# Decoder block, two layers: softmax sums on TensorE, one exponential per bank, layer normalisation on ScalarE

## The reference, cut to what matters

```python
def _layernorm(x, axis=-1, eps=1e-05):
    m = jnp.mean(x, axis=axis, keepdims=True)
    v = jnp.var(x, axis=axis, keepdims=True)
    return (x - m) / jnp.sqrt(v + eps)

# third block ("pick"): the 50 tokens with the largest gate attend to each other, 16 heads of 16
scores = jnp.einsum('bqhd,bkhd->bhqk', q, k) / jnp.sqrt(jnp.float32(dh))
attn = jax.nn.softmax(scores, axis=-1)
o = jnp.einsum('bhqk,bkhd->bqhd', attn, v).reshape(B, C, D) @ Wo

# fourth block ("local"): 100 tokens, 16 heads of 16, keys up to 64 positions away
scores = jnp.where(valid[None, None], scores, -jnp.inf)
probs = jax.nn.softmax(scores, axis=-1)
ctx = jnp.einsum('bhtw,bhtwd->bhtd', probs, vb)
```

## Time and profile before

| what | value |
|---|---|
| median of 3 runs | 1005.72 us (1004.74 to 1008.41) |
| profiled execution, its own time | 1008.58 us |
| its span, first to last instruction | 1006.8 us |
| mean granted TensorE clock | 0.917 of full speed |
| busy: PE, DVE, ACT, POOL | 863.1, 664.2, 506.9, 377.1 us |
| instructions: PE, DVE, ACT, POOL | 7003, 2065, 2373, 528 |

### The profile page before, as it was taken

How to read it: one execution, slowest core, us unless ns; L and a number is a source line. 1 busy time by engine, 2 the same in 40 slices (tenths; PEclk the granted TensorE clock), 3 DMA queues, 4 the chain that set the end, 5 groups by cost and what they waited for, 6 DMA issues and landing times. The chain is left out here.

```text
span 1006.8 us, 19701 instructions
## 1 busy us (share of the span) xinstructions
PE 863.1 (86%) x7003; PEld 642.6 (64%) x7003; DVE 664.2 (66%) x2065; ACT 506.9 (50%) x2373; POOL 377.1 (37%) x528
## 2 busy tenths in 40 slices
PE   8899889887985898998696899899797798999893
PEld 5567867455763676755575687666476577776572
DVE  5396656547888574555588875466858775665687
ACT  3042475864332437577333346568553444767741
POOL 0483024335544212324553431243635341233343
PEclk9999889879997989979798899899898898999996
DMA  7870000000441000000343100000322200000001
GB/s 232 282 251 1 2 2 1 2 24 24 164 150 66 9 2 2 2 1 25 116 145 112 39 2 2 2 1 25 109 93 78 87 25 1 2 1 2 1 1 33
DMA packets 22942, 53.28 MB, mean 53 GB/s; under 512 B 3656, under 2 KB 9548, under 8 KB 22844
## 3 DMA queue, kind: packets, MB, share of 16 engines
q1 hardware_dynamic: 22844, 52.02, 15.6%
HBM read 48.71 MB, written 3.31 MB: 52 GB/s over the span
## 5 line engine op out<-in xcount | busy, mean ns | idle before, releaser
L790 ACT ACTIVATE work<-psum,mx 100x100 f32<-100x100 f32 x512 | 171.5, 390 | 32.4 <-DVE mx L1075 32.2
L790 ACT ACTIVATION_READ_ACCUMULATOR work<-psum,mx 100x1 f32 x512 | 127.0, 254 | 0.0
L688 ACT ACTIVATE xT<-psum 128x100 f32<-128x100 f32 (+3 forms) x144 | 54.1, 381 | 127.7 <-PE psum L425 46.9
L1196 POOL COPY work<-rden 100x128 f32<-100x128 f32 (+1 forms) x80 | 25.1, 313 | 222.6 <-DVE rden L1079 149.9
L1167 POOL TENSOR_SCALAR ve<-mv 100x2 f32<-100x2 f32 x96 | 22.2, 231 | 228.1 <-DVE mv L915 227.7
L472 PE MATMUL psum<-eT,ctx 128*128 128x100 f32 x768 | 97.0, 281 | 2.8 <-DVE eT L942 2.6
L472 PEld LDWEIGHTS psum<-eT,ctx 128*128 128x128 f32 x768 | 93.3, 197 | 6.0 <-DVE eT L942 4.5
L920 DVE TENSOR_SCALAR x<-res,mv,rstd 100x256 f32<-100x256 f32 x160 | 81.9, 554 | 17.7 <-POOL rstd L1169 17.4
L688 ACT ACTIVATE eT<-psum 100x400 f32<-100x400 f32 (+3 forms) x128 | 65.3, 522 | 54.9 <-PE psum L655 28.2
L458 PE MATMUL psum<-ctxT,qT 128*100 128x361 f32 x256 | 89.8, 495 | 3.7 <-ACT qT L703 3.0
L1075 DVE TENSOR_REDUCE mx<-psum 100x4 f32<-100x400 f32 x128 | 67.0, 567 | 26.0 <-PE psum L619 25.9
(11 more groups left out here) (232 smaller groups left out, 1994.2 us busy)
## 6 DMA issues: line engine op xcount, KB each, us to landing
ctx<-in_ctx SPq DMA_DIRECT2D x16, 768.0 KB, 7.4
ctxT<-in_ctxT SPq DMA_DIRECT2D x16, 722.0 KB, 5.6
cell<-in_cell SPq DMA_DIRECT2D x12, 282.0 KB
seq<-in_seq SPq DMA_DIRECT2D x12, 282.0 KB
x<-in_x SPq DMA_DIRECT2D x16, 200.0 KB
out<-xplus SPq DMA_DIRECT2D x16, 200.0 KB
eT<-agent_rows SPq DMA_DIRECT2D x12, 200.0 KB
work<-in_x SPq DMA_DIRECT2D x4, 400.0 KB
```

Of the source, the lines that this page charges most:

```text
L688: return e.activation(dst, src, ACT.Copy, **kw)
L790: last = e.activation(s.e[:, h, :], bk[g][0:S, q * S:(q + 1) * S], ACT.Exp, bias=s.mx[0:S, h:h + 1], accum_out=s.den[0:S, h:h + 1])
```

## The change

Four things are edited, and the strings of `ORDER` for all five engines are new.

1. In local attention the way of the sums over GpSimd is gone. Behind the products of `eT` with `v` into `bk[0]`, TensorE makes the same 8 products with a tile of zeros and ones (`sums`, written once) into `bk[1]`, which gives each head's sum on the partitions of that head. VectorE takes the reciprocal of these 128x100 values straight from PSUM and multiplies. The exponentials no longer sum. A transpose, a spread and a copy on ScalarE go.
2. In the stage of the chosen tokens VectorE adds the negated maximum to a whole bank of scores (128x400) and writes the result to `e_pick`; ScalarE takes one exponential of it; VectorE adds up the columns of each head. There are two banks.
3. `normalize` is on ScalarE: `res * rstd + shift`, with two operands that hold one value for each partition. GpSimd makes `shift = -mean * rstd` in two instructions of one column each, behind `rstd`. `shift` lies in the tile `ez`, and so its name in the order is `ez`.
4. The maxima of the two banks in local attention are two steps, where they were one. The spread of the local sums is gone from GpSimd, and the steps `blocks` are given out one by one.

```diff
+                    e.wait_ge(*act(f"eT{i}", t))
                     e.wait_ge(*dve(f"eT{i}", t))
-                    e.wait_ge(*pool(f"re{i}", t))
-                    e.transpose(bk[1][:, 0:S], s.rspread, ident[0:S, 0:S]).then_inc(*pe.up(f"R{i}"))
-                    e.wait_ge(*act(f"eT{i}", t))
-                    for j in range(2):
-                        for r in range(ROWS):
-                            h = 2 * r + j
-                            last = e.matmul(bk[0][32 * r:32 * r + 32, 0:S], s.v[0:S, b, c * HQ + h, :],
-                                            s.eT[0:S, h * S:(h + 1) * S], start=j == 0, stop=j == 1, skip_group_check=True)
+                    for bank in range(2):
+                        for j in range(2):
+                            for r in range(ROWS):
+                                h = 2 * r + j
+                                last = e.matmul(bk[bank][32 * r:32 * r + 32, 0:S],
+                                                sums[:, j, :] if bank else s.v[0:S, b, c * HQ + h, :],
+                                                s.eT[0:S, h * S:(h + 1) * S], start=j == 0, stop=j == 1, skip_group_check=True)
                     last.then_inc(*pe.up(f"av{i}"))
...
             e.memset(minus_half[:, :], -0.5)
+            for j in range(2):
+                for k in range(2):
+                    e.memset(sums[:, j, k * DH:(k + 1) * DH], float(j == k))
             e.memset(token_w, 0.0)
             for part in key_w:
...
+            def normalize(act, pool, t, dst):
+
+                for b in range(NB):
+                    e.wait_ge(*pool(f"nm{b}", t))
+                    e.activation(dst[0:S, b, :], s.res[0:S, b, :], ACT.Identity, scale=s.rstd[:, b:b + 1],
+                                 bias=s.shift[:, b:b + 1]).then_inc(*act.up(f"x{b}"))
+
             def tokens_columns(t, pe, act):
...
-                    for i in range(4):
-                        for j in range(2):
-                            at_ = (2 * i + j) * CAP
-                            h = HQ * (i // 2) + 2 * (2 * (i % 2) + g) + j
-                            last = e.activation(s.e_pick[:, 4 * g + i, j, 0:CAP], bk[g][:, at_:at_ + CAP], ACT.Exp,
-                                                bias=s.mx[:, h:h + 1], accum_out=s.den[:, h:h + 1])
-                    last.then_inc(*act.up(f"ex{g}"))
+                    e.wait_ge(*dve(f"su{g}", t))
+                    part = s.e_pick[:, 4 * g:4 * g + 4, :, 0:CAP]
+                    e.activation(part, part, ACT.Exp).then_inc(*act.up(f"ex{g}"))
                     yield
...
-                    for g in range(2):
-                        e.wait_ge(*dve(f"m{'ab'[g]}{i}", t))
-                        for q in range(4):
-                            h = 4 * g + q
-                            last = e.activation(s.e[:, h, :], bk[g][0:S, q * S:(q + 1) * S], ACT.Exp,
-                                                bias=s.mx[0:S, h:h + 1], accum_out=s.den[0:S, h:h + 1])
-                        last.then_inc(*act.up(f"ex{'ab'[g]}{i}"))
-                        yield
+                    e.wait_ge(*dve(f"ma{i}", t))
+                    for h in range(0, 4):
+                        last = e.activation(s.e[:, h, :], bk[0][0:S, h % 4 * S:(h % 4 + 1) * S], ACT.Exp,
+                                            bias=s.mx[0:S, h:h + 1])
+                    last.then_inc(*act.up(f"exa{i}"))
+                    yield
+                    e.wait_ge(*dve(f"mb{i}", t))
+                    for h in range(4, 8):
+                        last = e.activation(s.e[:, h, :], bk[1][0:S, h % 4 * S:(h % 4 + 1) * S], ACT.Exp,
+                                            bias=s.mx[0:S, h:h + 1])
+                    last.then_inc(*act.up(f"exb{i}"))
+                    yield
                     e.wait_ge(*pe(f"tra{i}", t))
                     copy(s.eT[0:S, 0:4 * S], bk[0][0:S, 0:4 * S]).then_inc(*act.up(f"eT{i}"))
                     yield
-                    e.wait_ge(*pe(f"R{i}", t))
-                    copy(s.xT[:, 0, 0:S], bk[1][:, 0:S]).then_inc(*act.up(f"R{i}"))
-                    yield
                 if t + 1 < TURNS:
                     masks_log(e, s, t + 1)
                     yield
+                normalize(act, pool, t, s.x)
+                yield
 
                 yield from cross(t, "second", bqk)
...
 
-            def normalize(dve, pool, t, dst):
-                e.wait_ge(*pool("rstd", t))
-                for b in range(NB):
-                    e.tensor_scalar(dst[0:S, b, :], s.res[0:S, b, :], s.mv[:, b, 0:1], s.rstd[:, b:b + 1], ALU.subtract,
-                                    ALU.mult).then_inc(*dve.up(f"x{b}"))
-
...
+                def of_bank(stat, g):
+                    return stat[:, :].rearrange("p (i g j) -> p g i j", g=2, j=2)[:, g, :, :]
+
                 for g in range(2):
-                    e.tensor_reduce(s.mx[:, :].rearrange("p (i g j) -> p g i j", g=2, j=2)[:, g, :, :],
-                                    bk[g][:, 0:4 * S].rearrange("p (i j k) -> p i j k", i=4, j=2), AX, ALU.max,
-                                    negate=True).then_inc(*dve.up(f"mx{g}"))
-                yield
-                e.wait_ge(*act("ex1", t))
+                    scores = bk[g][:, 0:4 * S].rearrange("p (i j k) -> p i j k", i=4, j=2)
+                    e.tensor_reduce(of_bank(s.mx, g), scores, AX, ALU.max, negate=True).then_inc(*dve.up(f"mx{g}"))
+                    e.wait_ge(*dve(f"mx{g}", t))
+                    e.tensor_tensor(s.e_pick[:, 4 * g:4 * g + 4, :, 0:CAP], scores,
+                                    of_bank(s.mx, g).unsqueeze(3).to_broadcast([P, 4, 2, CAP]), ALU.add).then_inc(
+                        *dve.up(f"su{g}"))
+                    yield
+                for g in range(2):
+                    e.wait_ge(*act(f"ex{g}", t))
+                    e.tensor_reduce(of_bank(s.den, g), s.e_pick[:, 4 * g:4 * g + 4, :, 0:CAP], AX, ALU.add).then_inc(
+                        *dve.up(f"sm{g}"))
+                    yield
+                e.wait_ge(*dve("sm1", t))
                 e.reciprocal(s.rden[:, :], s.den[:, :]).then_inc(*dve.up("rd"))
...
-                    e.reciprocal(s.rden[0:S, 0:HQ], s.den[0:S, 0:HQ]).then_inc(*dve.up(f"rd{i}"))
+                    e.tensor_reduce(s.mx[0:S, 0:4], bk[0][0:S, 0:4 * S].rearrange("p (h k) -> p h k", k=S), AX,
+                                    ALU.max, negate=True).then_inc(*dve.up(f"ma{i}"))
+                    yield
+                    e.tensor_reduce(s.mx[0:S, 4:8], bk[1][0:S, 0:4 * S].rearrange("p (h k) -> p h k", k=S), AX,
+                                    ALU.max, negate=True).then_inc(*dve.up(f"mb{i}"))
+                    yield
                     e.wait_ge(*pe(f"trb{i}", t))
                     e.tensor_copy(s.eT[0:S, 4 * S:8 * S], bk[1][0:S, 0:4 * S]).then_inc(*dve.up(f"eT{i}"))
                     yield
-
-                    e.wait_ge(*act(f"R{i}", t))
                     e.wait_ge(*pe(f"av{i}", t))
+                    e.reciprocal(s.xT[:, 0, 0:S], bk[1][:, 0:S]).then_inc(*dve.up(f"rd{i}"))
+                    e.wait_ge(*dve(f"rd{i}", t))
                     e.tensor_tensor(s.aT[:, c, b * S:(b + 1) * S], bk[0][:, 0:S], s.xT[:, 0, 0:S], ALU.mult).then_inc(
                         *dve.up(f"aT{i}"))
...
                 e.tensor_scalar(s.vare[:, :], s.mv[:, :, 1], LN_EPS, None, ALU.add).then_inc(*pool.up("ve"))
                 e.wait_ge(*pool("ve", t))
                 e.tensor_tensor(s.rstd[:, :], s.vare[:, :], minus_half[0:S, 0:NB], ALU.pow).then_inc(*pool.up("rstd"))
+                e.wait_ge(*pool("rstd", t))
+                for b in range(NB):
+                    e.tensor_scalar(s.shift[:, b:b + 1], s.mv[:, b, 0:1], s.rstd[:, b:b + 1], -1.0, ALU.mult, ALU.mult).then_inc(*pool.up(f"nm{b}"))
 
...
+                add_row(s.gpsimd["local"], s.scalar["pick"], t, bo1)
                 yield
                 for i in range(NB * NC):
-                    if i + 1 < NB * NC:
-                        blocks(t, i + 1)
-                        yield
-                    spread(s.gpsimd["local"], f"re{i}", s.vector["local"](f"rd{i}", t), s.rspread, S, HQ)
+                    blocks(t, i)
                     yield
                 if t + 1 < TURNS:
                     masks_product(e, s, t + 1)
...
 ORDER = {
     "PE": (
-        "ABCDABABACBAACBBAADCABADBDBBDCDCCCCDDADDCAAABBACDBCADABDDACABCADBABCBDDAACDBABCCADCDBAACABACBBDCAABD"
...
+        "CADBCACACABCBCCBCDCADCAABDBAAABBDDBBCDDDDCACBACDAABCDBABDCCBADCBADABCDDCBADABDCBCCADACBAACBDBBDCCABC"
```

142 lines of the change are left out of this document (67 added, 75 removed).

## The result

| | before | after |
|---|---|---|
| median of 4 runs, same chip | 1007.07 us (1004.74 to 1011.16) | 942.47 us (938.32 to 946.40) |
| profiled execution, span | 1006.8 us | 936.5 us |
| mean granted clock | 0.917 | 0.947 |

The ratio is 0.9354, with an interval of 0.9299 to 0.9409. The new strings, which I set at 0, are worth 54 on top (51 by the ratios, which take out the chip). The two don't simply add up: on the code of before the same strings lose 23 us.

What follows compares the result with a forecast made beforehand. TensorE was taken as the bound, busy 863 of 1007 us. Its work +21, VectorE's full stretches -28, ScalarE and chains -5, GpSimd's wait +5 and clock -5 gave -12: 994 us from 1005.7, range 964 to 1027.

Steps and rivals of the forecast that it cites:

- The new strings: Step orders of all engines: could not be priced from rows, set at 0, with 10 us either way.
- All that this change can gain must come out of those 144 us: TensorE, the bound, is idle for 144 us; any gain must come from there, as it gets more work.
- the clock: TensorE's granted clock: fewer waits in stretches below full speed give back 5 us, between 0 and 10.
- TensorE +21: Local attention: 512 new products of 39.1 us replace 64 transposes of 18.4 us, adding 21 us.
- TensorE near 880 busy: Sign that the forecast is right: TensorE's busy time near 880 us in the changed kernel.
- VectorE full, -28: Seven stretches with VectorE 80% busy: moving normalisation to ScalarE saves 28 us, between 14 and 46.
- rival 2: Normalisation was hidden or only changes its queue; full stretches give 14 to 16 us: no change, 1005 us, chance 0.18.
- Reciprocals +37 of VectorE: Local attention: 64 reciprocals of 100 columns instead of 8, 0.76 us each, add 37 us to VectorE.
- Rival 1: VectorE's longer reciprocals in local attention hold up other streams' maxima and copies: slower, 1025 us, chance 0.32.
- ScalarE -42, -5 in all for the local chain: ScalarE's work falls by 42 us; shorter waits and chains, less a longer loop chain, save TensorE 5 us.
- GpSimd +44 busy, +5: Two one-column instructions per normalisation add 44 us busy on GpSimd; the added wait costs TensorE 5 us.
- rival 3: The full stretches dissolve: all 46 us of VectorE's normalisation count and the clock gives 10: 970 us, chance 0.14.

Runs made afterwards that it cites:

- sums_twice: Changed kernel, order untouched, with the products of the local exponentials with the ones issued twice (512 more products): 957.4 us, ratio 0.9483.
- undo_norm: Changed kernel with its strings carried over and normalisation back on VectorE, the other edits kept: 953.3 us, ratio 0.9431.
- oldcode_ownstrings: Kernel before, code word for word, with new step sequences found by a search for that code: 939.9 us, ratio 0.9347.
- cheap_reciprocal: Changed kernel, order untouched, with each of the 64 local reciprocals of 128x100 replaced by a copy of the same tile: 937.3 us, ratio 0.9268.
- the control: Kernel before with its own strings passed through the same carrying over, which moves a few steps by a place or two: 1006.0 us, ratio 0.9908.

## Why the prediction was wrong, step by step

**The step that failed** is "The new strings. They re-time every step. I can't price them from rows; they stand at 0, with 10 us either way". On the changed code they are worth 54 us (996.9 to 942.5), against 10 at most. On the old code other strings are worth 38 to 68. All my rivals varied the edits, and none the strings; so the range held no more than those 10 us for them. The reasoning that a rewritten order has no price because no row names it was the fault: 144 us of idle time, with every engine but TensorE below 70%, is itself a row that leaves room for an order to give much.

**"All that this change can gain must come out of those 144 us"** was wrong in kind. 51 us came from there; TensorE's busy time fell by 19 more, where I had it rise by 21. The identical 7003 instructions had 863.1 us at 0.917 and 833.2 at 0.961, and the product of the two is nearly the same (791 and 801 us), so this part goes with the clock. I gave the clock 5 us and 10 at most.

**TensorE +21.** The new group has 33.9 us, that with `v` 35.3 instead of 39.1, so it is +30.1 - 18.4 = +11.7 by records. On the path 512 such products cost 15 us (sums_twice), and the transposes were not undone by themselves. The term was of the right size and a little high. "TensorE near 880 busy" failed with the clock, at 843.9.

**VectorE full, -28.** This reading fell. VectorE's load was moved (76 us by undo_norm, where I counted 97), but putting it back costs 10 us with carried strings, and with own strings gains 18 in one pair and costs 12 in the other. The 10 us gap was one of order, and oldcode_ownstrings loses 41 us of TensorE's idle time with the normalisation where it was. undo_norm's 10 us lie below the 14 to 16 of rival 2. The sign of this edit couldn't be settled with two searches a side.

**Reciprocals +37 of VectorE.** Right: 775 ns measured, 764 forecast; from 32 to 100 columns 433 ns, 6.4 ns a column. Rival 1, the reciprocals decide, is refuted: VectorE's load in the local stretches did rise to the 73% that it reckoned with (72% measured), but the scores stand idle for 0.1 us in all, and cheap_reciprocal gives back 5 to 9 us for 33 of work.

**ScalarE -42, -5 in all for the local chain.** Reads of the sums: 51 us forecast, 44.6 measured; chosen tokens: 54 forecast, 60 measured by undo_bank. But normalisation takes 594 ns and not 420, so 104.6 us instead of 81, one instruction at my upper bound of 595. ScalarE fell by 18 us and not 42. The use of these was far too small: I gave the shorter exponentials 4 us by TensorE's 11.0 us wait, and the 512 reads alone cost 19; I gave the chosen tokens 3, and undone they cost 18 with carried strings and 8 with their own. By my terms the edit of the local sums was a loss, +21 - 5 = +16 us; undone, it costs 38 and 46. The 19 us of the reads are one part of that; no run parts the rest. How a small wait in front of TensorE can be worth so much wasn't tested. My reading is that the wait on a page is what the other streams have left uncovered, and that with a tight order less work is left to cover with.

**GpSimd +44 busy, +5.** 281 ns instead of 231 for each of the one-column instructions, 50.9 us. What it costs was not measured apart from undo_norm's 10 us, which holds it.

**The sum.** -12 for the code, measured -15 (-7 to -21) on the old strings. Against the control it is -9, and 0 isn't excluded, so this agreement is weak. Part of it is luck, since in it a term that fell (-28) stands against two that were too small. Rivals 2 and 3 were made of the same terms; rival 3 came nearest of all at 970 us, but by VectorE's normalisation, which the runs don't bear out.

## What to carry to other kernels

When a change comes with a new order of the steps, price the order first and give it a range of its own: its bound is the idle time of the bounding engine, plus what the clock gives back when the idle time goes (41 and 30 us in oldcode_ownstrings), and not what the edits' instructions add up to. An order belongs to its code: the same strings gained 54 us on one code and lost 23 on the other, so an edit is judged only with an order cut for it, and by more than one. Before calling an engine full because it is busy 80% where the bounding engine idles, look in order of time at what it stands at inside that stretch.
